# The last pair of image chunks of the patch embedding computed by seven products instead of eight

## The reference

```python
def tokens_of(X, W, b, class_token, pos_embed):          # the stage of this case
    patches = X.reshape(B, 3, 8, 28, 8, 28).transpose(0, 2, 4, 1, 3, 5).reshape(B, 64, 2352)
    tokens = jnp.einsum('bpi,hi->bph', patches, W) + b    # 2352 -> 128
    tokens = jnp.concatenate([cls, tokens], axis=1)       # 65 tokens an image
    return tokens * pos_embed[None, :, :]

def reference(x, ...):                                    # x: (128, 3, 224, 224) float32
    h = tokens_of(x, ...)
    h = h + attention_0(layernorm(h))
    h = h + experts_0(layernorm(h))
    h = h + attention_1(layernorm(h))
    h = h + experts_1(layernorm(h))
    return h
```

## Time and profile before

| what | value |
|---|---|
| median of three runs | 1677.53 us |
| the profiled execution | 1674.36 us, of which span of the trace 1672.6 us |
| TensorE (matmul) busy over the span | 1588.6 us, 95% |
| VectorE, ScalarE, GpSimd busy | 1242.1, 911.3, 784.6 us |
| last pair by eight products, TensorE | from 215.41 to 247.64 us |
| first product of the layer norm | at 249.42 us |

### The profile page before, as it was taken

How to read it: one execution, slowest core, us unless ns; L and a number is a source line. 1 busy time by engine, 2 the same in 40 slices (tenths; PEclk the granted TensorE clock), 3 DMA queues, 4 the chain that set the end, 5 groups by cost and what they waited for, 6 DMA issues and landing times. The chain is left out here.

```text
span 1672.6 us, 62551 instructions
## 1 busy us (share of the span) xinstructions
PE 1588.6 (95%) x24380; PEld 1171.9 (70%) x24380; DVE 1242.1 (74%) x3629; ACT 911.3 (54%) x2406; POOL 784.6 (47%) x932
## 2 busy tenths in 40 slices
PE   7999998999999999997999988999999999869997
PEld 3333334777777787785667746888887888669997
DVE  2799916888888888885776763677777777768875
ACT  0112325666666667663454455666666667447753
POOL 0000000888888888884011112345555555645554
PEclk9999999999999999999899999999999999879999
DMA  9999940000000000001200000000000000035431
GB/s 337 355 374 356 353 156 1 3 4 4 4 4 3 4 4 3 4 3 38 78 1 1 1 1 6 3 12 19 28 21 22 21 21 21 34 115 152 133 85 41
DMA packets 73078, 118.06 MB, mean 71 GB/s; under 512 B 11627, under 2 KB 30366, under 8 KB 72828
## 3 DMA queue, kind: packets, MB, share of 16 engines
q1 hardware_dynamic: 65054, 100.04, 18.2%
q0 software_dynamic: 6096, 12.94, 2.2%
q10 hardware_dynamic: 1678, 1.43, 0.3%
HBM read 97.59 MB, written 18.61 MB: 69 GB/s over the span
## 5 line engine op out<-in xcount | busy, mean ns | idle before, releaser
L1692 PE MATMUL ps<-xn,s_a_wqkv 128*128 128x260 f32 x1024 | 277.0, 402 | 6.1 <-DMA s_a_wqkv<-in_f_b 3.0
L1692 PEld LDWEIGHTS ps<-xn,s_a_wqkv 128*128 128x128 f32 x1024 | 178.0, 192 | 51.5 <-issue 18.1
L1033 POOL TENSOR_TENSOR prob_a<-e_a,inv_sum_a 128x512 f32<-128x512 f32 x64 | 66.9, 1046 | 194.7 <-issue 113.3
L1558 DVE TENSOR_REDUCE neg_max_a<-ps 128x8 f32<-128x520 f32 x128 | 89.2, 697 | 71.9 <-PE ps L1666 49.0
L2308 POOL DMA_INDIRECT out<-h,xn x93 | 97.6, 1049 | 90.4 <-DVE h L2423 86.6
L1776 PE MATMUL ps<-s_a_wqkv,xn_pair_a 128*64 128x256 f32 x1024 | 138.8, 392 | 0.0
L1088 ACT ACTIVATE resT_a<-ps 128x260 f32<-128x260 f32 x256 | 85.2, 386 | 96.6 <-PE ps L1743 59.7
L1017 POOL TENSOR_TENSOR kept_a<-e_a,keep_a 128x585 f32<-128x585 f32 x64 | 87.2, 1362 | 69.2 <-issue 59.1
L918 POOL MEMSET cls_queries_a<- 128x1040 f32 x2 | 1.9, 966 | 249.0 <-POOLq L430 249.0
L1743 PE MATMUL ps<-probT_a,horner_a 64*64 64x65 f32 x2048 | 113.0, 227 | 1.7 <-DVE horner_a L1304 1.5
L1733 PE MATMUL ps<-horner_a,probT_a 64*64 64x64 f32 x2048 | 106.5, 220 | 2.9 <-issue 2.9
(11 more groups left out here) (305 smaller groups left out, 4632.8 us busy)
## 6 DMA issues: line engine op xcount, KB each, us to landing
x_chunk<-in_x_main SPq DMA_DIRECT2D x144, 512.0 KB, 11.1
xn<-pair_rows SPq DMA_DIRECT2D x93, 130.0 KB, 2.2
pair_rows<-pad_rows_m SPq DMA_DIRECT2D x29, 130.0 KB
s_f_all<-in_f_w SPq DMA_DIRECT2D x2, 1024.0 KB
x_ends<-in_x_tail SPq DMA_DIRECT2D x16, 96.0 KB, 5.9
out<-h,xn POOLq DMA_INDIRECT x93
s_w_tok<-in_w_tok SPq DMA_DIRECT2D x6, 192.0 KB, 8.7
pair_rows<-rows_m,slot_i_m POOLq DMA_INDIRECT x65, 2.5
```

The source lines that it names most:

```text
L1558: last = nc.vector.tensor_reduce(neg_max[:, :, 0:CH], score(), AX.X, ALU.min)
L1692: nc.tensor.matmul(ps[:, QK_BANK[i], 0:QUAD], w_qkv[:, c * P:(c + 1) * P], xn[:, t.h * QUAD:(t.h + 1) * QUAD], start=True, stop=True).then ...
```

## The change

Pair 7 goes through `seven_products` as well, so `terms`, `fourth_term` and `ends_gap` run for it too, and the joins of pair 6 move in among them. Its partial results are taken out in another manner than those of pairs 1 to 6: ScalarE copies 7 halves and then leaves, and a new function `last_join` has VectorE copy two halves itself, form two sums straight out of PSUM, do the remaining additions, some of them in halves, and the two finishes.

```diff
@@ tensor
             eight_products(0)
-            for p in range(1, last_pair):
+            for p in range(1, pairs):
                 if p == 2:
                     pe.wait_ge(tok_done, 2)
                 since(pe, evicted, COPIES * (p - 2))
@@
-            pe.wait_ge(evicted, COPIES * (last_pair - 2))
-            eight_products(last_pair)
@@ scalar, evict(p)
                 for dst, src in ((three_seven[lo], b[lo]), (three_seven[hi], d[hi]),
-                                 (five_seven[lo], c[lo]), (five_seven[hi], d[lo]),
-                                 (six[lo], c[hi]), (six[hi], c[hi]), (one[lo], a[hi]), (one[hi], a[hi]),
+                                 (five_seven[lo], c[lo]), (five_seven[hi], d[lo])):
+                    copy(dst, src).then_inc(evicted, 1)
+                if p == last_pair:
+                    copy(two_four[lo], a[lo]).then_inc(evicted, 1)
+                    copy(two_four[hi], b[hi]).then_inc(evicted, 1)
+                    copy(five[hi], c[lo]).then_inc(evicted, 1)
+                    return
+                for dst, src in ((six[lo], c[hi]), (six[hi], c[hi]), (one[lo], a[hi]), (one[hi], a[hi]),
                                  (two_four[lo], a[lo]), (two_four[hi], b[hi]), (five[hi], c[lo])):
                     copy(dst, src).then_inc(evicted, 1)
@@
             for p in range(1, last_pair):
                 evict(p)
                 copy_u2(p)
+            evict(last_pair)
@@ vector
+            def last_join():
+                p = last_pair
+                a, b, c, d = (ps[:, 4 * (p % 2) + i, :] for i in range(4))
+                done = 5 * (p - 1)
+                dve.wait_ge(step_done, HK * (p + 1))
+                dve.wait_ge(tok_done, 2 * p)
+                for dst, src in ((one[lo], a[hi]), (one[hi], a[hi])):
+                    nc.vector.tensor_copy(dst, src).then_inc(own_copied, 1)
+                dve.wait_ge(own_copied, 2)
+                for side in (lo, hi):
+                    nc.vector.tensor_tensor(six[side], one[side], c[hi], ALU.add).then_inc(joined, 1)
+                dve.wait_ge(evicted, COPIES * (p - 1) + 4)
+                nc.vector.tensor_tensor(five_seven[:, :], three_seven[:, :], five_seven[:, :], ALU.add)\
+                    .then_inc(joined, 1)
+                dve.wait_ge(joined, done + 3)
+                nc.vector.tensor_tensor(three_seven[:, :], five_seven[:, :], six[:, :], ALU.add).then_inc(joined, 1)
+                dve.wait_ge(evicted, COPIES * (p - 1) + 6)
+                dve.wait_ge(joined, done + 4)
+                nc.vector.tensor_tensor(one[lo], one[lo], two_four[lo], ALU.add).then_inc(joined, 1)
+                nc.vector.tensor_tensor(one[hi], three_seven[hi], two_four[hi], ALU.add).then_inc(joined, 1)
+                dve.wait_ge(evicted, COPIES * (p - 1) + 7)
+                nc.vector.tensor_tensor(three_seven[hi], three_seven[hi], five[hi], ALU.add).then_inc(joined, 1)
+                dve.wait_ge(joined, done + 6)
+                finish(2 * p, one[:, :])
+                dve.wait_ge(joined, done + 7)
+                finish(2 * p + 1, three_seven[:, :])
@@
-            for m in range(HK, last_pair * HK):
+            for m in range(HK, pairs * HK):
...
-            fourth_term(last_pair * HK - 1)
+            fourth_term(pairs * HK - 1)
             for part in range(2, 7):
-                join(last_pair - 2, part)
-            for part in range(7):
                 join(last_pair - 1, part)
-            finish_classic(last_pair)
+            last_join()
```

More of the change, by code:

```diff
@@ L97, in patch_embed @@
         evicted, joined, u2_copied = sem("parts_evicted"), sem("parts_joined"), sem("u2_copied")
+        own_copied = sem("parts_copied_dve")
         tok_done, cls_done = sem("tok_done"), sem("cls_done")
@@ L323, in finish_classic @@
             def finish_classic(p):
-                dve.wait_ge(tok_ps, 1 + p // last_pair)
+                dve.wait_ge(tok_ps, 1)
                 for c in range(2):
                     finish(2 * p + c, ps[:, 4 * (p % 2) + c, :])
+            def last_join():
[24 more added lines that the diff above has]
+                finish(2 * p + 1, three_seven[:, :])
             def add(out, a, b):
```

## The result

The changed kernel takes 1684.45 us (median of 10 runs, 1679.35 to 1689.96), the kernel before in the same session 1677.72 (10 runs, 1674.07 to 1681.23); the ratio is 1.0044 [1.0031, 1.0056]. I had predicted 1680 us, +0.24%, and most of my chance lay on "no change that a measurement can tell". The time is inside the range, but the difference can be told from nothing: the forecast of "the same" failed.

What follows compares the result with a forecast made beforehand. TensorE was taken as the usual limit, alone at work in pair 7. A 2.63 us later layer norm start plus 1.45 us of low clock made 4.1 us on a base of 1676.0, so 1680 us; range 1675.5 to 1684.5.

Steps and rivals of the forecast that it cites:

- the forecast of "the same": Whole kernel: 1680 us, about 0.24% slower, within the 0.3% a measurement can tell from no change; chance 0.67.
- TensorE's saving: Pair 7 by seven products hands over at 243.75 us instead of 247.69, 3.94 us sooner.
- pair 7 was fed as argued: VectorE's 26.7 us of work fits a pair of 28.2, with a lead of 5.4; VectorE too slow: chance 0.03.
- The tail: Behind pair 7's last product: eleven VectorE instructions take 7.98 us instead of 1.41, range 7.3 to 8.8.
- The start of the layer norm: Stage before the layer norm ends 2.63 us later: 3.94 us gained and 6.57 lost.
- What the pause does to the clock: Layer norm after a pause of some 8.3 us: low clock makes the variance 1.45 us late, by the dense restarts.
- The long low clock: Rival, first 6 us of the layer norm: 2.6 us lost instead of 1.45, 1681.2 us; chance 0.28 with the long tail.
- The local sum: Later layer norm start plus low clock: 2.63 + 1.45 = 4.1 us more.
- The later stages: Everything behind the layer norm's first product follows in a chain and moves by the same amount.
- a sign of being wrong: Listed signs: tail below 6 us, layer norm losing over 3 us, or a later stage moving differently from the first.
- theory B: Experiments' theory: the rest of the program loses more when it starts at another time or in another condition.
- The base: Time of the kernel before: mean of four executions, 1676.0 us, to which the sum was added.

Runs made afterwards that it cites:

- e6_late_first: Changed kernel with bank a's products (pair 7, steps 1 to 8) issued last, so most joining runs under the products; 1.0048 of the kernel before.
- e9_late_again: e6_late_first once more, unchanged, with more executions; 1.0047 of the kernel before.
- e4_again: Changed kernel once more, no edit, more runs; 1680.14 us against 1674.54 for the kernel before, 1.0035.
- e5_no_tail: Changed kernel with last_join replaced by two finishes and ScalarE's last copies left out (last 16 images wrong); 0.9992 of the kernel before.
- e10_busy5: Kernel before with five unused full-width products on TensorE behind pair 7; 1.0041, +6.9 us.
- e7_late_centers: e6_late_first with the pause filled by three unused products and the layer norm's first three centered blocks; 1.0018 of the kernel before.
- e1_warm: Changed kernel with nine unused full-width products keeping TensorE busy through the tail; 1.0026 of the kernel before, +4.4 us.
- e2_pause: Kernel before with nine unused, chained VectorE additions behind the last finish, giving the pause alone; 1.0052, +8.7 us.
- e3_busy: Kernel before with seven unused full-width products on TensorE behind pair 7; 1.0047, +7.9 us.
- the two busy kernels: e3_busy and e10_busy5: kernel before with seven or five unused products behind pair 7; 1.0047 and 1.0041.

## Why the prediction was wrong

*TensorE's saving* (forecast 3.94 us): 4.41, right. The page's full stretch at 192 us is unchanged, and pair 7 was fed as argued: VectorE waited for loads 2.3 us in all up to 243 us, 1.5 at most, and TensorE's 28 us covered it. ScalarE's copies of pair 6 moved from 215.52 to 221.48 us, behind the finishes of pair 5, as told, and nobody waited for them; VectorE waited 0.69 us for the twelfth copy, as before.

*The tail* (7.98, range 7.3 to 8.8): 7.88, right, and from the right instructions. A copy and a sum from PSUM take no longer than those from SBUF (0.68 to 0.69 us each), and ScalarE kept its distance of 4.28/7 = 0.61 us while VectorE read PSUM beside it. That reading one bank at once costs nothing is shown only for some 0.4 us, in which both read halves of bank c. The rule of the Trainium skill (page "VectorE: DVE Perf Modes", section "Two Vector instructions with no wait between them") held where I had not followed it: L355, in the same half as L353 before it, started 0.61 us behind it (248.41 to 249.02), while L353, which changes the half, was 0.71 us behind L352. The sum by the rule was 7.85.

*The start of the layer norm* (+2.63 us): +2.06. The difference is the 0.47 us of the earlier hand-over and the 0.10 of the tail.

*What the pause does to the clock* is the term of the sum that was mis-sized: "I take 1.45, by the dense restarts." The long low clock, priced at 2.6 us and given 0.28 with the long tail, is what came: 2.32, 2.50 and 2.51 us in three profiles with a pause of 8.2 us, where the clock came back 5.4, 6.2 and 6.1 us after the restart. (How the prediction got to 2.6 does not come out of its rows: a fourth block done at 5.64 us makes the variance 5.64 - 3.31 = 2.33 us late, and no row gives the "6.4 instead of 3.8".) The traces of before had three restarts, and I sorted them by how dense the work behind them was. But at the restarts at 838.88 and 1480.94 the clock had been low for 14 and 28 us, from before the idle times named in the earlier trace rows; only the one at 1005.89 shows a clock that fell with its pause.

```profile
834.00:838.00 4.00, 2.32 (x10) 2.13 (x10) 2.20 (x12) 1.51 (x4) 0.00 (x0) 0.50 0.00 0
...
1454.00:1470.00 16.00, 10.06 (x41) 7.15 (x40) 12.07 (x75) 6.59 (x20) 8.96 (x9) 0.50 0.19 67
```

And the density of the work is not what makes the price: in e6_late_first and e9_late_again one kernel shows both, 1.34 and 2.35 us. I had treated as a property of the work what differs between executions. The Trainium skill says this of the clock (page "TensorE: Matmul & The Clock Gate", section "The HAM clock gate (the "warmup" mystery)"): how many of the first products run cold differs from run to run of one kernel. The two traces of that kernel agree.

The local sum came out all the same, +4.4 us of the forecast +4.1, and that is luck: the start was 0.57 us too late in the forecast and the clock 0.87 us too cheap. By itself it makes 0.26% and would still have been "the same".

*The later stages* are the step that carried the time over the 0.3%: "all later stages follow in a chain and move by the same amount". The prediction put their difference at nothing, without a row for it, and had named it as a sign of being wrong. In the first profile the delay grew from 4.4 us at the milestone to 14.7 at the end of the span; in e4_again, the same kernel, it shrank from 4.8 to 2.9. In the mean of the first ten executions 2.3 us [0.1 to 4.3] are left for it. I had also not thought of the *time outside the span*: +0.7 us in the first session, +0.3 in the second. On average it was 2.0 to 2.5 us in the kernels with seven products in the last pair and 1.8 in those with eight; the cause is not shown. Local shift and time outside the span come to 5.1 us in both sessions, where +7.4 [5.2, 9.4] and +5.9 [3.3, 8.4] were measured: the second needs no more, the first 0.1 us or more. But e5_no_tail, e6_late_first and e9_late_again lie above theirs, milestone and time outside the span together (-4.8, +3.1 and +4.0 us), by more than their intervals allow.

Two kinds of low stretches behind the layer norm were seen in the traces, at the entry to the attention (5.1 us in e10_busy5) and in the attention itself (3.4 us at 340 us in the first profile, and more at 790). Whether they make up the rest can be estimated from the clocks of all executions. Within the kernel before, 0.001 less of mean clock went with 1.1 to 1.3 us more of span (three sessions). At that price the clocks of the table and the later start of the layer norm (in e7_late_centers of its first variance) cover the mean spans of e4_again, e1_warm and e2_pause to within 0.9 us. In the six others 1.4 to 3.8 us stay open. 0.001 of mean clock is 3.3 us at half the clock; if each of them cost the full half, 1.7 us, some 2 to 3 us would still stay open in e3_busy, e5_no_tail and e10_busy5. So theory B is not refuted for these: either low stretches move there to places where they cost more, or the later stages lose time by something else. No run here parts the two.

*The base.* That draws are wide is shown by the kernel before itself: 31 executions on one chip had spans from 1665.7 us at a mean granted clock of 0.982 to 1680.6 at 0.973, with a correlation of -0.91 between the two. I took the mean of four executions and the profile of one; the sign was safe, a decision at 0.3% was not.

## What to carry to other kernels

A step that shortens TensorE's work and lengthens what stands between it and its next work is paid twice: once for the tail, and once for the clock that falls in the longer pause (here 4.4 us saved, 6.5 and 2.3 to 2.5 paid). Price the clock after a new pause by the worst restart of the trace and not by the one whose work looks alike, and do not count on the thin places behind it (little work between two waits) passing at full clock as they did so far. When the expected difference is below the spread of the executions, look at the granted clock of all of them before a single profile is believed.

## What was not expected of the hardware

- The same kernel with the same pause of 4.40 us lost 1.34 us to the clock in one execution and 2.35 in another.
- A place with idle times of 0.46 and 0.66 us ran at 2.4 GHz in some kernels (1.99 us for eight products) and at 1.2 GHz in others (3.81). In the two busy kernels the work and the waits right before it were those of the kernel before; in the other three one wait was longer, 1.30 us instead of 0.88.
- Around the pauses of 8.2 us the clock was low for 10.2 us in all, in three executions, 5.4 to 6.2 of them after the restart with dense products.
- Behind the pause of 4.40 us the clock fell, in one execution, only when TensorE had been at work again for one us.
